# Value products of the last attention heads in three fp32r parts instead of one fp32 product, the newest convolution tap on ScalarE, and one buffer for the output weights

## The reference, cut to what matters

```python
def _mamba(x, ...):
    xs, z = jnp.split(x @ W_in.T, 2, axis=-1)
    xs = silu(causal_conv(xs, conv_w) + conv_b)      # 4 taps per channel
    ...                                              # dt, B, C; scan over time with 16 states
    return y * silu(z) @ W_out.T

def _xattn(x, latents, ...):                         # x: context, latents: the tokens
    q = ln @ Wq; k, v = split(concat([xn, ln]) @ Wkv)    # 16 heads of 64, 2113 keys
    w = softmax(q k^T / 8); return (w @ v) @ Wout

x = layernorm(x + _mamba(x)); x = layernorm(x + _xattn(ctx_1024, x)); x = layernorm(x + _ffn(x))
```

## Time and profile before

| | |
|---|---|
| time, median of 3 runs | 3115.12 us (3111.74 to 3118.14) |
| the profiled execution: its own time | 3116.32 us |
| its span | 3114.6 us |
| stretch of `prepare` / of attention before head 0 | 0 to 152.9 / 152.9 to 308.6 us |
| batch 0, 1, 2 and 3 of the head loop | 597.9, 597.1, 596.2 and 557.1 us |
| what follows | 457.7 us |

### The profile page before, as it was taken

One profiled execution on the slowest core, in us unless ns is written; L12 is line 12 of the kernel. 1 busy time (PEld: TensorE's weight loads), 2 busy tenths in 40 slices (PEclk: granted clock), 3 DMA queues, 4 the chain that ended last, 5 costly groups with the idle time before them and its releaser, 6 DMA issues. The chain is left out here.

```text
span 3114.6 us, 33965 instructions
## 1 busy us (share of the span) xinstructions
PE 2951.2 (95%) x11610; PEld 1849.9 (59%) x11610; DVE 1951.6 (63%) x3381; ACT 1347.4 (43%) x2318; POOL 1084.6 (35%) x850
## 2 busy tenths in 40 slices
PE   7577999999999999999999999999999999899996
PEld 3234565656565656566666666665656565676665
DVE  5897777775667777756777775655555454452225
ACT  4653545453545454435454554454343434211121
POOL 4495667660017675500466663000000000102213
PEclk9898999999999999999999999999999999799998
DMA  6352312111122121201221122101010100411112
GB/s 221 145 180 92 92 35 59 35 56 52 38 69 65 35 58 35 82 18 51 70 65 58 35 62 59 38 13 40 15 38 14 38 15 14 169 60 51 55 43 68
DMA packets 71679, 189.84 MB, mean 61 GB/s; under 512 B 8420, under 2 KB 39272, under 8 KB 63448
## 3 DMA queue, kind: packets, MB, share of 16 engines
q1 hardware_dynamic: 67096, 172.08, 18.2%
q0 software_dynamic: 3984, 15.60, 1.6%
q10 hardware_dynamic: 432, 0.01, 0.0%
HBM read 124.59 MB, written 28.44 MB: 49 GB/s over the span
## 5 line engine op out<-in xcount | busy, mean ns | idle before, releaser
L1100 ACT ACTIVATE a_carry<-a_st 128x512 f32<-128x512 f32 (+1 forms) x1088 | 649.4, 597 | 1125.5 <-PE a_st L1528 1117.1
L1540 PE MATMUL a_o<-a_carry,a_vals 128*65 128x512 f32 (+1 forms) x2176 | 1113.7, 593 | 0.0
L1277 DVE TENSOR_REDUCE a_maxes<-a_mx 128x1 f32<-128x512 f32 x1016 | 678.0, 686 | 224.6 <-PE a_mx L1451 217.1
L1528 PE MATMUL a_st<-a_q,a_kone 65*128 65x512 f32 (+1 forms) x1088 | 431.9, 397 | 0.0
L961 POOL TENSOR_TENSOR a_shared<-a_shared,a_bc 128x512 f32<-128x512 f32 x192 | 251.6, 1311 | 385.1 <-DVE a_shared L1217 385.1
L1540 PEld LDWEIGHTS a_o<-a_carry,a_vals 128*65 128x65 f32 (+1 forms) x2176 | 284.2, 137 | 103.7 <-issue 1.8
L1527 PE MATMUL a_st<-a_q,a_keven 128*128 128x512 f32 (+1 forms) x544 | 326.1, 599 | 1.4 <-ACT a_q L1079 0.9
L932 POOL TENSOR_TENSOR a_erstd<-a_emv,a_half 128x4 f32<-128x4 f32 x7 | 7.1, 1014 | 892.4 <-DVE a_emv L1303 892.4
L1527 PE MATMUL a_st<-a_q,a_kodd 128*128 128x512 f32 (+1 forms) x544 | 314.9, 579 | 0.0
L1451 PE MATMUL a_mx<-a_kodd,a_q 128*128 128x512 f32 x512 | 298.1, 598 | 9.2 <-DVE a_maxes L1277 8.3
L1217 DVE TENSOR_TENSOR_SCAN a_shared<-a_shared 128x512 f32<-128x512 f32 x192 | 288.5, 1505 | 14.5 <-POOL a_shared L950 13.1
(11 more groups left out here) (267 smaller groups left out, 4437.6 us busy)
## 6 DMA issues: line engine op xcount, KB each, us to landing
a_bc<-m_kept_bc SPq DMA_DIRECT2D x48, 512.0 KB, 3.7
a_wt<-a_w_split SPq DMA_DIRECT2D x15, 1536.0 KB, 9.1
a_kone<-a_keven SPq DMA_DIRECT2D x32, 528.5 KB, 4.5
a_kone<-a_kodd SPq DMA_DIRECT2D x32, 528.5 KB, 4.3
e_wall<-in_w_t_dram SPq DMA_DIRECT2D x27, 512.0 KB, 9.8
a_shared<-m_kept_bc SPq DMA_DIRECT2D x16, 512.0 KB, 3.6
a_w_split<-a_wt POOLq DMA_DIRECT2D x4, 1536.0 KB, 6.3
a_shared<-in_ctx_dram SPq DMA_DIRECT2D x4, 1536.0 KB
```

The source lines that it names most:

```text
L1100: nc.scalar.activation(p_of(s % 4)[0:r], st[0:r, s % 2], ACT.Exp, scale=SCALE).then_inc(exp_done, 1)
L1277: nc.vector.reduce_max(maxes[:, c, t:t + 1], mx_bank(g, i), AX_X).then_inc(mx_max, 1)
L1528: nc.tensor.matmul(st[0:r, s % 2], k_one[g % 2][0:DH + 1, kt * P:kt * P + r], qm[of(g)][0:DH + 1, :], start=False, stop=True).then_inc(st_ ...
L1540: nc.tensor.matmul(ps_o[0:DH + 1, g % 2], vals[0:r, kt * HG + j, :], p_of(s % 4)[0:r], start=(kt == 0), stop=(kt == KT - 1)).then_inc(pv_d ...
```

## The change

Three edits.

1. For all 272 tiles of the last batch, and for tiles 0 to 11 of heads 12 to 15 in the three others (144 tiles), the value product is done as three fp32r products. ACT makes a rounded copy `p_high` of the exponentials after each such exponential, POOL subtracts it to make `p_low`, and the values are kept as `vals_high` (rounded by ACT) and `low_last` or `low_some` (made by DVE). `p_high` lies where the Mamba data in `a_carry` were, `p_low` where `a_bc` is. So the next batch's data are fetched only after the last value product of the batch before (batches 1 and 2), and the scan units of the next batch stand 6 slots later there.
2. In `prepare`, ACT multiplies the newest tap straight from PSUM, and DVE's round of four taps becomes three rounds.
3. The output weights have one place, and are fetched at slot 10 of a group's first head.

```diff
+                wait_full(act, ("x", i, c))
+                nc.scalar.activation(cv[:, c], bank(("x", i, c)), ACT.Copy, scale=cw[:, c, DC - 1:DC])
                 nc.scalar.activation(xs_pad[:, c, DC - 1:], bank(("x", i, c)), ACT.Copy).then_inc(front_read, 1)
...
-                    if j == 0:
-                        ins = nc.vector.tensor_scalar(cv[:, c], tap, w, None, ALU.mult)
-                    else:
-                        ins = nc.vector.scalar_tensor_tensor(cv[:, c], tap, w, cv[:, c], ALU.mult, ALU.add)
+                    ins = nc.vector.scalar_tensor_tensor(cv[:, c], xs_pad[:, c, j:j + S], cw[:, c, j:j + 1], cv[:, c],
+                                                         ALU.mult, ALU.add)
...
+def unit_slot(b, u):
+    return int(u * U_STEP) + (6 if b > 0 else 0)
...
+LAST = (B - 1) * H
+SOME = 12
+def is_split(g, kt):
+    return g >= LAST or g % H >= H - HG and kt < SOME
...
-        wo_sb = sb("a_wo", [P, 2, HG, DM + 1])
+        wo_sb = sb("a_wo", [P, HG, DM + 1])
...
             def load_batch(b):
                 sp.wait_ge(turned_low, b * len(PREP))
+                if b > 1:
+                    sp.wait_ge(pv_done, (b - 1) * H * KT)
...
+                    if g % HG == 0 and g > 0 and kt == 10:
+                        sp.wait_ge(ring_full, AT["O", g - 1, TT - 1] + 1)
+                        load_wo(g // HG)
...
+            def low_exp(g, kt):
+                n, r, p = SPLIT[g, kt], tile_rows(kt), p_of((g * KT + kt) % 4)
+                pool.wait_ge(p_high_ready, n + 1)
+                nc.gpsimd.tensor_tensor(p_low(n)[0:r], p[0:r], p_high(n)[0:r].bitcast(F32), ALU.subtract).then_inc(p_low_ready, 1)
...
             def high(what):
+                else:
+                    act.wait_ge(pv_done, (n * HG - 1) * KT + t + w)
+                    a = nc.scalar.activation(vals_high[0:r, t * HG:(t + w) * HG, 0:DH],
+                                             ring[0:r, k, 0:w * GW].rearrange("p (a d) -> p a d", d=DH), ACT.Copy)
...
                 if s >= 4:
                     act.wait_ge(pv_done, s - 3)
+                    if divmod(s - 4, KT) in SPLIT:
+                        act.wait_ge(p_low_ready, SPLIT[divmod(s - 4, KT)] + 1)
                 nc.scalar.activation(p_of(s % 4)[0:r], st[0:r, s % 2], ACT.Exp, scale=SCALE).then_inc(exp_done, 1)
+                if divmod(s, KT) in SPLIT:
+                    act.wait_ge(exp_done, s + 1)
+                    nc.scalar.activation(p_high(SPLIT[divmod(s, KT)])[0:r], p_of(s % 4)[0:r], ACT.Copy).then_inc(p_high_ready, 1)
...
+                    if has_split(what):
+                        o = nc.vector.tensor_tensor(vals_low(n)[0:r, t * HG:(t + w) * HG], made, own[:, :, 0:DH], ALU.subtract)
...
             def add_o(s):
+                if (g, kt) in SPLIT:
+                    n, high, low = SPLIT[g, kt], vals_high[0:r, kt * HG + j, :], vals_low(g // HG)[0:r, kt * HG + j]
+                    pe.wait_ge(p_high_ready, n + 1)
+                    nc.tensor.matmul(ps_o[0:DH + 1, g % 2], high, p_high(n)[0:r], start=(kt == 0), stop=False)
+                    nc.tensor.matmul(ps_o[0:DH, g % 2], low, p_high(n)[0:r], start=False, stop=False)
+                    pe.wait_ge(p_low_ready, n + 1)
+                    nc.tensor.matmul(ps_o[0:DH + 1, g % 2], high, p_low(n)[0:r], start=False, stop=(kt == KT - 1)).then_inc(pv_done, 1)
+                    return
```

More of the change, by code:

```diff
@@ L620, with has_split @@
 BANK, RANK = ring_banks()
-HIGH = {x: i for i, x in enumerate(x for x in MADE if x[0] in "QK")}
+LAST = (B - 1) * H
+SOME = 12
+def is_split(g, kt):
+    return g >= LAST or g % H >= H - HG and kt < SOME
+SPLIT = {}
+for tile in ((g, kt) for g in range(NH) for kt in range(KT) if is_split(g, kt)):
+    SPLIT[tile] = len(SPLIT)
+def has_split(what):
+    return what[0] == "V" and is_split(what[1] * HG, VB[what[2]][0])
+HIGH = {x: i for i, x in enumerate(x for x in MADE if x[0] in "QK" or has_split(x))}
 POW = {x: i for i, x in enumerate(x for x in MADE if x[0] in "EGLg" or x[0] == "A" and x[2] == 1)}
@@ L633, in sem @@
             return ctx.enter_context(nc.semaphore(name))
+        with ExitStack() as later:
+            p_high_all = later.enter_context(nc.sbuf_tensor("a_phigh", [P, 2, CT, S], F32R))
+        p_high = lambda n: p_high_all[:, n % 4 // 2, n % 2]
         carry = sb("a_carry", [P, 2, CT, S])
         y = sb("a_y", [P, CT, S])
+        with ExitStack() as later:
+            p_low_all = later.enter_context(nc.sbuf_tensor("a_plow", [P, CT, S], F32R))
+        p_low = lambda n: p_low_all[:, n % 4]
         bc_gate = sb("a_bc", [P, CT, S])
+        with ExitStack() as later:
+            low_last = later.enter_context(nc.sbuf_tensor("a_lowlast", [P, KT * HG, DH], F32R))
         shared = sb("a_shared", [P, CTX_T * DM + 2 * TT * DM])
```

51 lines of the change are left out of this document (32 added, 19 removed).

## The result

The changed kernel takes 3103.64 us, the median of 13 runs (3094.03 to 3111.08), against 3115.12 before (3111.09 to 3118.14): ratio 0.9961, 95% interval 0.9953 to 0.9970. It is faster, but the forecast was 3068 in a range from 3042 to 3096, so the time is 36 us above the forecast and 8 outside the range. The profiled execution took 3111.08 us (span 3109.3) and is the slowest of the 13, so what the trace shows is somewhat worse than the median.

A forecast was written before the change was run, and what follows sets the result against it. PE, 99% busy in the head loop, was taken as the bound. Gains of 38.7 us in the last batch, 6.5 in the others and 4 from taps, less 2 for starts, made 47: 3068 us, range 3055 to 3083, with rivals 3042 to 3096.

The forecast's parts named there:

- The saving of 0.17 a tile: Value product: three fp32r parts take 0.69 us instead of 0.86; 46.2 us in the last batch, 24.5 in the others.
- Rival D: Value products of 64 or 65 columns take 0.29 us instead of 0.23, so nothing is gained: 3113 us; chance 0.04.
- rival A: Everything is hidden; queues give back only the odd heads' 0.34 us: 70 us less, 3045 us; chance 0.10.
- GpSimd in the last batch: Subtractions of 1.27 us each there, with the low part in time for PE three slots later.
- Rival C: POOL sets the pace, its subtraction taking 2.20 us throughout: 44 us lost in the last batch, 3160 us; chance 0.05.
- Odd heads of the last batch: Slots 0 to 5: late key copies on ACT give back 0.75 us per head, 5.3 us in seven heads.
- the head's end: The row of maxima waits behind slot 15's rounded copy on ACT: 0.1 us in 15 heads, 1.5 us given back.
- Head 14: In batches 0 to 2, ACT's work gives back 3.2 us and the port 1.3 per head; 13.5 us in three heads.
- Heads 13 and 15: Odd heads before the last batch: 0.75 us of the split's saving given back each, leaving -1.25 us per head.
- Starts of batches: Batches 1 and 2: later data fetches make ACT and DVE's scan wait; 1 us each (0 to 4), 2 us lost.
- The taps: In `prepare`, the second batch's projection begins at about 29.5 instead of 32.19; 4 us gained (2 to 6).
- Rival B: ACT paces more than head 14, so all give-backs double: 20 us less, 3095 us; chance 0.15.

The follow-up runs named there:

- e4: The changed kernel with GpSimd's subtraction over 8 columns instead of 512 in every split tile, third product over the high part, low part left out: 3079.81 us, ratio 0.9895.
- e3: The changed kernel with the split only in the last batch, keeping the shift of the scan units and SP's wait: 3087.43 us, ratio 0.9916.

## Why the prediction was wrong

**The step that failed** is what GpSimd's new subtractions do to VectorE in the heads before heads 16, 32 and 48. The prediction put them at 1.3 us in each of heads 14, 30 and 46 and at nothing in the others: 3.9 us. With the subtractions shortened (e4), the trace is 26.0 us shorter in these heads and the median 23.8 us lower, out of 36 that the forecast was off. Of the 26.0, 10 to 12 us are TensorE's clock, for which the sum had no term at all.

The sum, term by term, in the profiled executions; 41.9 us are missing (47.2 forecast, 5.3 found).

- *The saving of 0.17 a tile* is right: every slot without a stall is 0.16 to 0.17 shorter, head 50 took 26.33 us, and the value products begin 0.23 apart in threes. Rival D is gone with it, and rival A with the stalls below.
- *GpSimd in the last batch* is right: 345.95 us over 271 operations is 1.28, and PE did not wait for it. Rival C is gone.
- *Odd heads of the last batch*: 0.75 given back each (and 0.1 at the head's end); 1.2 and 1.9 measured, mostly in slot 4. The mechanism was right (with the copy gone from ACT's way 4 to 5 us came back) and the size about half. With the first head of each group, which gave back 0.5 (head 48 1.1) where 0.1 was charged, and head 63, which did better by 0.4, this is 6.0 us.
- *Head 14.* ACT was charged 3.2 and the port 1.3 ("bounds 0 and 27 x 0.5"). Without the long GpSimd instructions the head stood at +0.2, so ACT's part is 2.2. The port's is 5.0, about 1.5 of it clock, inside the bounds but four times the term, for which no working is given. 5 of 15 normalisations lost about 1 us each and a sixth 0.4. VectorE has time to spare in that head (23.4 us busy of 33.6), but PE waits for just these rows, so the loss is not taken up. The Trainium skill ("SBUF — State Buffer", SBUF: two separate sides), cited for this in the prediction, says that whichever starts first holds the pair for the whole instruction. The traces agree: the six long normalisations end 0.15 us after GpSimd's instruction does, and with quarter instructions the eleven of the first line take 0.54 us on average instead of 0.80. The prediction quoted the rule, but did not count which operations start under a subtraction, or how long one holds them.
- *Heads 13 and 15*: -1.25 forecast, -1.0 and -1.4 without the port's stalls. In heads 13, 29 and 45 the first of the four row operations (L1376) of the Mamba norm lost 0.9 us to GpSimd, in slot 4, where PE waits for maxima already (1.65 us in e4); that made the waits of 2.56 us.
- *The clock has no term at all.* Six stretches at half clock cost about 13 us in the trace (15.4 at most): some 3 each in heads 16, 29 and 45, 1.5 each in 14, 30 and 46. The trace of before had shown no wait over 0.8 us in the loop and full clock all through; an estimate that lets PE wait 2 us at a stroke has to reckon with nearly twice that. This is about a third of what is missing in the profiled execution, nearly as much as GpSimd's hold on VectorE without the clock (26.0 less 10 to 12), and some 8 us in the median run by the estimate above; it goes with the spread of 17 us.
- *Starts of batches*: 1 us each; 7.5 and 1.5 measured. Shift and wait alone gave 1.7 and 1.2 (e3); the rest goes with a later landing at head 16, whose cause is open, and the clock. *Shifted units*: no term; 1.8 and 3.5 in the profile, 6.1 with the starts in medians.
- *The taps*: 4 forecast, 4.8 to head 0. PE waited 0.80 us before the second projection instead of 4.12; it began at 29.92 where 29.5 was forecast, and took 7.10 at full clock instead of 10.12:

```profile
22.01 7.11 PE L404 MATMUL m_ring<-m_xt,m_win 128*128 128x512 f32 x16
29.92 7.10 PE L404 MATMUL m_ring<-m_xt,m_win 128*128 128x512 f32 x16 [0.80 <-ACT a_bc L280]
```

Rival B came nearest (3095) for the wrong reason, which is luck: it let ACT pace, and PE hardly waited for ACT's exponentials. The prediction's own signs of being wrong (a head with j = 2 over 27.5 us, PE waiting for POOL in the last batch) did not show, since they looked only at the last batch; the sign that did was head 14, with 38.8 us instead of 34 to 36 and with PE waiting for VectorE and not for ACT. The range was too narrow because its worse end doubled the named terms and had no room for one that was missing.

## What to carry to other kernels

Where TensorE is 99% busy and hardly waits, price a new wait by its longest single stroke, not by its sum: here about 2 us of standing still cost 1.5 to 3 us again in clock, about every second time. Where GpSimd and VectorE both work from SBUF, what counts is how long one GpSimd instruction is and how many VectorE operations start under it; cutting the instruction in four brought back 12 us (11 measured from before each time) although GpSimd became busier. And a saving that must borrow buffers from another stage (a shift, a later load) should be tried first only where it borrows nothing: that alone was 22 us better than the whole change.
